# Attention on one core: weighings of two key tiles joined, and maximum products set between the halves of the scores

## What is computed

```python
xn = _group_norm(xf, gamma, beta)
qkv = jnp.einsum('oc,bcl->bol', w_qkv, xn) + b_qkv[None, :, None]
q, k, v = jnp.split(qkv, 3, axis=1)
weight = jnp.einsum('bct,bcs->bts', q * scale, k * scale)
weight = jax.nn.softmax(weight.astype(jnp.float32), axis=-1).astype(q.dtype)
a = jnp.einsum('bts,bcs->bct', weight, v)
hid = jnp.einsum('oc,bcl->bol', w_proj, a.reshape(b, c, L)) + b_proj[None, :, None]
return (xf + hid).reshape(b, c, h, w)
```

## Time and profile before

| | |
|---|---|
| median of 3 runs | 2491.03 us (2490.61 to 2492.5) |
| the profiled execution's own time | 2492.64 us |
| its span in the trace | 2491.1 us, granted PE clock 0.99 on the mean |
| PE busy | 2438.5 us, 98% |
| DVE, ACT, POOL busy | 1615.9, 1150.5, 1182.5 us |
| maximum products, PE matmuls (two groups, L1509) | 1024 matmuls, 120.0 and 115.1 us |
| scores, PE matmuls (L1539) | 3200, 417.8 us |
| weighings, PE matmuls (L1558) | 2048, 495.7 us |

### The profile page before, as it was taken

The page is one execution under the profiler, slowest core; times in us unless marked ns, Lnnn a source line. Parts: engine busy times, 40 slices in busy tenths (PEclk is TensorE's granted clock), DMA queues, the critical chain, the costliest instruction groups (busy, mean ns, idle before and its releaser), DMA issues. The chain is left out here.

```text
span 2491.1 us, 37555 instructions
## 1 busy us (share of the span) xinstructions
PE 2438.5 (98%) x12980; PEld 1615.9 (65%) x12980; DVE 1615.9 (65%) x2161; ACT 1150.5 (46%) x1499; POOL 1182.5 (47%) x590
## 2 busy tenths in 40 slices
PE   8999999999799999999999999999999999999988
PEld 7888888788655566557556655755665575557544
DVE  6455555455667766775777577567857756775776
ACT  3332233223355645654555456355555645553553
POOL 3330000000047665773766667377656755771762
PEclk8999999999899999999999999999999999999999
DMA  6431111013221242215122321512231241213002
GB/s 199 139 111 45 56 67 66 27 42 128 83 95 35 111 144 88 109 32 211 34 97 104 130 101 53 194 43 102 93 144 34 110 175 63 97 31 119 26 26 76
DMA packets 73401, 226.75 MB, mean 91 GB/s; under 512 B 12224, under 2 KB 12224, under 8 KB 72384
## 3 DMA queue, kind: packets, MB, share of 16 engines
q1 hardware_dynamic: 58720, 172.01, 19.6%
q0 software_dynamic: 14560, 52.96, 5.8%
HBM read 141.05 MB, written 71.30 MB: 85 GB/s over the span
## 5 line engine op out<-in xcount | busy, mean ns | idle before, releaser
L591 POOL TENSOR_TENSOR a_all<-a_all 128x1024 f32<-128x1024 f32 x410 | 1010.1, 2464 | 508.2 <-ACT a_all L816 473.3
L816 ACT ACTIVATE a_all<-psum 128x1024 f32<-128x1024 f32 x512 | 496.5, 1022 | 80.3 <-PE psum L1539 67.7
L1104 DVE TENSOR_REDUCE small<-psum 128x2 f32<-128x1024 f32 x326 | 399.6, 1226 | 172.3 <-PE psum L1509 172.1
L1558 PE MATMUL psum<-a_all 128*64 128x512 f32 x2048 | 495.7, 605 | 0.0
L1311 PE MATMUL psum<-r_all 128*128 128x512 f32 x1920 | 454.5, 395 | 6.9 <-DVE r_all L1198 5.8
L1311 PEld LDWEIGHTS psum<-r_all 128*128 128x128 f32 x1920 | 359.4, 189 | 101.6 <-DVE r_all L957 10.2
L1539 PE MATMUL psum<-r_all 64*128 64x512 f32 x3200 | 417.8, 393 | 2.0 <-ACT a_all L816 2.0
L1498 PE MATMUL psum<-r_all 128*128 128x512 f32 x1536 | 364.4, 396 | 5.6 <-DVE r_all L1217 5.6
L1539 PEld LDWEIGHTS psum<-r_all 64*128 64x128 f32 x3200 | 301.7, 186 | 73.2 <-ACT a_all L816 14.0
L1498 PEld LDWEIGHTS psum<-r_all 128*128 128x128 f32 x1536 | 286.0, 189 | 85.9 <-issue 24.4
L1558 PEld LDWEIGHTS psum<-a_all 128*64 128x64 f32 x2048 | 124.0, 136 | 232.5 <-issue 173.4
(11 more groups left out here) (147 smaller groups left out, 2450.9 us busy)
## 6 DMA issues: line engine op xcount, KB each, us to landing
r_all<-w_dram SPq DMA_DIRECT2D x48, 1024.0 KB, 4.9
xn_dram<-a_all POOLq DMA_DIRECT2D x56, 512.0 KB, 7.0
r_all<-xn_dram SPq DMA_DIRECT2D x7, 4096.0 KB, 15.3
a_all<-y_dram SPq DMA_DIRECT2D x9, 2048.0 KB, 10.8
a_all<-x SPq DMA_DIRECT2D x16, 1024.0 KB, 6.5
y_dram<-a_all SPq DMA_DIRECT2D x16, 1024.0 KB, 4.2
out<-a_all SPq DMA_DIRECT2D x32, 512.0 KB, 4.0
a_all<-sums SPq DMA_DIRECT2D x192, 64.0 KB, 2.0
```

What stands on the lines that cost most here:

```text
L591: pool.tensor_tensor(p_sum[:, :, cols], probs[:, 0, :, cols] if i == 1 else p_sum[:, :, cols], probs[:, i % SLOTS, :, cols], ALU.add).then ...
L816: act.activation(probs[:, i % SLOTS, :, cols], psum[half][:, :, :], ACT.Exp, scale=SCALE).then_inc(probs_ready, 1)
L1104: dve.reduce_max(max2[:, :, tile, half], psum[3][:, :, :], AX_X).then_inc(work_free, 2)
L1558: last = pe.matmul(psum[2][h * D:(h + 1) * D, half], v_t[:, i, head], probs[:, i % SLOTS, h, half * HALF:(half + 1) * HALF], start=(i == 0 ...
```

## The change

It does five things.

- PE's loop goes over two key tiles at a time. The scores of a half are a call of their own. A maximum product stands between the two halves of each tile, one ahead of the first tile's scores (but for the first two tiles, where maximum product 0 stands there already) and one behind the second's. Then come the weighings of tiles i - 1 and i together. The pair ends with the weighing of tile 7, right behind those of 5 and 6.
- The sums stand behind the second half of tile 0 as before.
- `COPIED` is (2, 4, ..., 14), seven products, and no longer (3, 5, ..., 13), six. ACT copies product 2i ahead of tile i's exponentials.
- DVE inverts the sums behind products 3, 7 and 11 (two parts at the last), no longer behind 2, 4, 6 and 8.
- PE waits for the second half of the next queries (`qk_hi_done`) at maximum product 4 and no longer at 1.

```diff
-        COPIED = tuple(range(3, MAXES - 2, 2))
+        COPIED = tuple(range(2, MAXES, 2))
...
-                        if more and 2 * i - 1 in COPIED:
-                            copy_max(pairs, 2 * i - 1)
+                        if more and 2 * i in COPIED:
+                            copy_max(pairs, 2 * i)
...
-                            if p and m in (2, 4, 6, 8):
-                                invert_sums(b, p - 1, m // 2 - 1, 1)
+                            if p and m in (3, 7):
+                                invert_sums(b, p - 1, m // CT, 1)
+                            if p and m == 11:
+                                invert_sums(b, p - 1, 2, 2)
...
-            def scores(pairs, par, i, more):
+            def scores(pairs, par, i, half, more):
...
-                            if m == 1:
+                            if m == CT:
 
                                 pe.wait_ge(qk_hi_done, (pairs + 2) * QK)
...
-                    for i in range(NT):
-                        scores(pairs, par, i, more)
-                        if p and more and i == 0:
-
-                            pe.wait_ge(k_free[1], pairs + 2)
-                            sums(pairs - 1, psum[2][:, 0])
+                    for i in range(0, NT, 2):
+                        if i:
+                            next_max()
+                        for tile in (i, i + 1):
+                            scores(pairs, par, tile, 0, more)
+                            next_max()
+                            scores(pairs, par, tile, 1, more)
+                            if p and more and tile == 0:
+
+                                pe.wait_ge(k_free[1], pairs + 2)
+                                sums(pairs - 1, psum[2][:, 0])
                         next_max()
-                        if i:
-                            weigh(b, p, i - 1, more)
-                            next_max()
+                        for tile in range(max(i - 1, 0), i + 1):
+                            weigh(b, p, tile, more)
                     weigh(b, p, NT - 1, more)
```

More of the change, by code:

```diff
@@ L1519, in v_tile @@
                                       for j in range(CT) for w, m in THREE]).then_inc(work_full, 1)
-            def scores(pairs, par, i, more):
+            def scores(pairs, par, i, half, more):
                 keys = slice(i * P, (i + 1) * P)
[L1523 to L1541, removed]
+                cols = slice(half * HALF, (half + 1) * HALF)
+                pe.wait_ge(probs_ready, ONE + pairs * 2 * NT + (2 * (i - 1) + half + 1 if i else 0))
+                if i == 0 and half == 0:
+                    pe.wait_ge(turn_read, pairs + 1)
+                    if more:
+                        pe.wait_ge(k_free[0], pairs + 2)
+                terms = [(k_hl[:, par, k, keys], q_hl[:, par, q, cols]) for k, q in ((HI, HI), (LO, HI), (HI, LO))]
+                if i == 0:
+                    terms.append((ones_r, mx[:, cols]))
+                for t, (k, q) in enumerate(terms):
+                    for h in range(2):
+                        rows_ = slice(h * D, (h + 1) * D)
+                        last = pe.matmul(psum[half][:, h], k[rows_], q[rows_], start=(i == 0 and t == 0),
+                                         stop=(t == len(terms) - 1), skip_group_check=(i > 0))
+                last.then_inc(scores_full, 1)
             def weigh(b, p, i, more):
```

## The result

The changed kernel takes 2558.89 us (median of 4 runs, 2556.72 to 2559.28) against 2491.77 of the kernel before (4 runs, 2490.61 to 2492.75): a ratio of 1.0267, 95% interval 1.0252 to 1.0283. It is 67 us slower; forecast were 80, a time of 2571 and a range of 2540 to 2593. The profiled execution took 2559.28, its span is 2557.8, and it ran at a mean granted clock of 0.993.

The account below looks back on a forecast made before the run. PE was taken as the bound, busy 98% of the span. 31 pairs at +2.58 us gave +80.0: 2492.6 + 80.0 = 2572.6, forecast as 2571 since the profiled execution stood 1.6 over the median; range 2540 to 2593.

Parts of the forecast that it names:

- the walk: Hand-summed PE steps and waits through one block of two key tiles: 8.54 us against 7.84 before.
- Product b: Maximum product between the even tile's halves: waits until a is read, starting 1.29 us behind it.
- a: Block's first maximum product, behind the weighings, now copied: its PSUM is free 1.23 us behind its start.
- c: Maximum product between the odd tile's halves: waits for DVE's reading of product b, starting 1.96 us behind it.
- d: Maximum product behind the odd tile's second half: waits until c is read, 1.29 us behind it; weighing 0.42 later.
- the POOL part of the text: POOL's 13 additions start later, end at 40.2; sums at a batch's end come at 41.6, covered with 1.4 left.
- The first: Rival: fewer switches between scores and weighings alone count, 0.37 us per removed group, 46 less, 2445; chance 4%.
- The second: Rival: products hardly wait, only exponentials do; block 8.08, about 0.9 a pair, 28 us more, 2519; chance 6%.
- The third: Rival: no measurable difference in the whole kernel, if half the waits went and the saving stayed; chance 2%.
- the fourth: Rival: waits feed each other through a lower clock or queued copies; 0.3 more a block, 2608; chance 7%.
- Pairs without sums I take alike: Pairs without sums were given the same +2.58 us, with the same waits or an exponential's instead of one.
- Last pair... I take 0: Last pair, without products: exponential waits of 2.2 us, set against PE's 2.38 idle behind it; 0, bounds 0 and 2.2.

Follow-up runs that it names:

- a_short_exp: The changed kernel with exponentials on 8 of the 512 columns per head and half: 2558.19 us, 1.0258 of the kernel before.
- a_short_reads: The changed kernel with DVE reading 8 of 512 columns per head of every maximum product and no ACT copies: 2492.76 us, 0.9998 of the kernel before.
- a_short_adds: The changed kernel with short product reads, no copies, short exponentials, and POOL's additions of tiles 2 to 7 on 8 of 512 columns: 2416.69 us.
- b_short_adds: The kernel before with short product reads, short exponentials and POOL's additions of tiles 2 to 7 cut to 8 of 512 columns: 2464.52 us.

## Why the prediction was right

**The block.** The products' starts stand in the trace as the walk had them. Product b 1.29 behind a (forecast 1.29), c 2.00 behind b (1.96), d 1.21 behind c (1.29), the weighing 0.40 behind d (0.42); a block 8.48 and 8.58 (8.54). For c and d the agreement is in part luck: the walk let DVE's reading release c, in the trace the exponential did, about 0.1 us later, and d came sooner by as much. The walk's own chain, seen in a_short_exp, has 1.88 and not 1.96 there. The odd tile's second half starts 3.68 behind a, forecast 3.85. The first block is 8.52 (8.53), product 1 at 1.89 (1.91). The stretch is 1331.31 to 1367.08, 35.77 (35.86). That product reading sets the block and the exponentials do not was the walk's claim; a_short_reads and a_short_exp show it. The granted clock stayed 1.00 in the stretch, and at an image's end the sums' matmul comes 5.71 behind the end of the last weighings (5.70 before), as the POOL part of the text expected.

**The rivals.** The first (switches alone, 2445) needs what only a_short_adds gives it, no reading and no exponential worth the name and short additions. Its price is real and as expected: a pair has four groups less and is 42.83 against 44.30 in those two runs, 0.37 a group. The Trainium skill, TensorEngine Tiling (Array Packing), Key Properties, says that a change of tiling mode drains TensorE. The traces agree in that such a change costs time; what TensorE does in that time they don't show. The second (exponentials only, a block of 8.08) is what a_short_reads shows when made true: 8.10. The third did not come. Of the fourth, the waits did not feed each other: the later blocks of a pair are 8.48 and 8.58, and the granted clock of the whole runs is 0.992 or 0.993, against 0.989 to 0.992 before.

**Where 13 of the 80 us went** (span against span, 66.7). The steps that were mis-sized:
- "Pairs without sums I take alike", +2.58. Measured +1.97: such a pair is 43.89 before and 45.86 after in most images, first product to first product. In the kernel before these 8 pairs already waited for exponentials behind tile 0, as its row shows below; a wait that was there cannot be paid again. About 4.5 us.

```profile
1397.78 1.88 PE L1539 MATMUL psum<-r_all 64*128 64x512 f32 x12 [0.30 <-ACT a_all L816]
```

- Pairs with sums, +2.58. Measured +2.40 (46.97 against 44.57): 2.49 of it in the stretch, and 0.09 back between the stretches. Some 3 us over the images 0 to 5 and the last.
- Image 6 ran badly in the profile of before: 46.90 and 46.28 for two of its pairs. In the first the next product waits 2.20, as its row below shows. In the second the loss is the granted clock: it was 1.00 up to 2155, is 0.50 in 2157 to 2160 right behind that wait, and the product, tile 0's scores and the sums take 4.87 where the earlier trace rows has 3.28. The changed kernel lost only 0.5 in each of these pairs, at a clock of 1.00. This made the difference smaller by about 4 us and is no part of the mechanism. In b_short_adds both pairs are 44.30; where the wait comes from in the others I did not find out.

```profile
2155.35 0.51 PE L1509 MATMUL psum<-u,r_all 64*128 64x512 f32 x2 [2.20 <-ACT r_all L694]
```

- "Last pair... I take 0". From the last image's third pair to the end the changed kernel is 0.5 shorter, where 2.6 were forecast for that third pair and 0 for the last. Ahead of the last pair PE waits for POOL anyway (6.20 before, 5.25 after), so 0.95 of the third pair's loss was covered. The last pair, between its sums, became 1.24 shorter: 1.08 ahead of its first weighing, where the clock came back sooner, and 0.16 behind it, where the exponentials' new waits and the shorter wait for DVE (0.51 for 2.38) all but cancel, as the text had taken. Behind the last sums another 0.7 are gone, at a clock of 0.94 and not 0.91.

```profile
2420.47 1.94 PE L1576 MATMUL psum<-a_all,small 128*32 128x512 f32 x8 [6.20 <-POOL a_all L591]
...
2428.13 1.94 PE L1558 MATMUL psum<-a_all 128*64 128x512 f32 x8
```

```profile
2489.13 1.93 PE L1577 MATMUL psum<-a_all,small 128*32 128x512 f32 x8 [5.25 <-POOL a_all L591]
...
2495.71 1.94 PE L1559 MATMUL psum<-a_all 128*64 128x512 f32 x8
...
2522.34 1.94 PE L1577 MATMUL psum<-a_all,small 128*64 128x512 f32 x8 [0.51 <-DVE a_all L1184]
```

Against these, 1.3 us were lost by a lower granted clock once (0.88 in 713.5 to 728 of the profile after, 1.00 before). So some 3.4 us of the 13 are the clock's, at three places of the kernel before, and 1.3 went the other way. All of this is smaller than the bounds, so the range held.

## What to carry to other kernels

Bunching like work to save switches crowds the engines that read its results: before joining, add up how long the one buffer between two producers is held (here 1.23 us for a copied product, where the next would come after 0.92 or 1.03, and 1.84 for a plain one, where it would come after 1.61) and compare it with the new spacing, not with the average load. A walk with start-to-start prices and each reader's own delay, a dozen steps by hand, gave each product's start in the block within 0.1 us, while busy shares (98% before, 97% after) told nothing. And shrinking the readers of one chain at a time, keeping the order, tells which of two interlocked chains binds: one took the whole loss away, the other nothing. Before a difference at a place where PE has just waited is put down to the order of work, the granted clock there should be compared.

## What was not expected of the hardware

- A wait of a matmul costs more than its length: a product that was released late held up the next piece by 0.42 where 0.33 is usual, since its weights were then loaded in its own time (in the weight loads' timeline the load starts with the matmul, and 0.2 ahead of it otherwise); the same shows for products between halves: 0.34 behind one that waited (1341.12 to 1341.46), 0.23 behind one that did not (1315.34 to 1315.57).
- ACT's and DVE's operations have small fixed parts here: 16 elements a partition took ACT 0.18 and DVE 0.17 to 0.18 us, against 1.03 and 1.23 for 1024.
- At a granted clock of 1.00, PE's distance from one piece to the next was the same in all kernels to 0.01 or 0.02 (two joined weighings 3.58 or 3.59 from their start to the next product in each), so the prices carried over from one order to another.
- A wait of PE can be followed by a second loss. Behind its wait of 6.20 the granted clock of the kernel before was 0.50 for another 5.9 us, and behind one of 5.25 in the changed kernel for 3.0, on the same work. Behind the wait of 2.20 in image 6 it was 0.50 in 2157 to 2160; behind that of 2.38 at 2454.92 it stayed at 1.00 up to 2460.
